# Last attention of a four-layer model: scores on 32-row tiles, value sums in nine rounds

## What is computed

```python
def _L3_attn_ref(x, W1, b1, W2, b2):
    y = jnp.einsum('bse,ef->bsf', x, W1) + b1
    y = y.reshape(B, S, H, -1).transpose(0, 2, 1, 3)
    q, k, v = jnp.split(y, 3, axis=-1)
    dk = jnp.asarray(v.shape[-1], x.dtype) ** 0.5
    w = jnp.einsum('bhqd,bhkd->bhqk', q, k) / dk
    mask = jnp.tril(jnp.ones((S, S), dtype=x.dtype))
    w = w * mask - NEG_BIG * (1.0 - mask)
    w = jax.nn.softmax(w, axis=-1)
    attn = jnp.einsum('bhqk,bhkd->bhqd', w, v)
    attn = attn.transpose(0, 2, 1, 3).reshape(B, S, E)
    return jnp.einsum('bse,ef->bsf', attn, W2) + b2
```

## Time and profile before

| | |
|---|---|
| runs | 1695.24, 1697.96, 1697.95 us |
| profiled execution | 1706.63 us, span 1704.9 |
| mean granted TensorE clock | 0.952 of 2.4 GHz |
| busy share of the span | PE 87%, DVE 74%, ACT 64%, POOL 50% |
| the stage that changes | from 1354 us to the end |

### The profile page before, as it was taken

How to read it: one execution, slowest core, us unless ns; L and a number is a source line. 1 busy time by engine, 2 the same in 40 slices (tenths; PEclk the granted TensorE clock), 3 DMA queues, 4 the chain that set the end, 5 groups by cost and what they waited for, 6 DMA issues and landing times. The chain is left out here.

```text
span 1704.9 us, 29946 instructions
## 1 busy us (share of the span) xinstructions
PE 1490.4 (87%) x11248; PEld 1197.3 (70%) x11248; DVE 1260.4 (74%) x2770; ACT 1089.9 (64%) x2122; POOL 857.1 (50%) x798
## 2 busy tenths in 40 slices
PE   6999999999999999899848888845999379998997
PEld 4788887888788887687737676834788256666675
DVE  6999999999999999435461677589433887777772
ACT  4888888888888888455445565632444456666665
POOL 4556576667666666720363744624666632233211
PEclk9999999999999999999779999957999699999999
DMA  3656666656666565300044000040465200000000
GB/s 94 124 103 115 106 120 100 120 108 114 115 108 103 99 105 106 87 1 1 18 137 129 26 2 2 2 133 1 112 148 109 64 1 1 2 2 2 2 2 26
DMA packets 334417, 117.09 MB, mean 69 GB/s; under 512 B 281008, under 2 KB 326096, under 8 KB 334144
## 3 DMA queue, kind: packets, MB, share of 16 engines
q1 hardware_dynamic: 323664, 101.54, 29.2%
q0 software_dynamic: 8496, 12.59, 3.4%
q10 hardware_dynamic: 2112, 1.05, 0.2%
HBM read 37.53 MB, written 10.49 MB: 28 GB/s over the span
## 5 line engine op out<-in xcount | busy, mean ns | idle before, releaser
L2135 ACT ACTIVATE ET_a<-PS 128x256 f32<-128x256 f32 (+2 forms) x512 | 220.5, 499 | 114.8 <-PE PS L2028 72.9
L771 POOL TENSOR_TENSOR dl<-XN,dh 128x1024 f16<-128x1024 f32 x86 | 184.9, 2150 | 155.2 <-DVE D L743 79.7
L205 PE MATMUL PS<-xh,yh 128*128 128x512 f32 x512 | 215.5, 421 | 6.6 <-ACT XNT L608 3.8
L206 PE MATMUL PS<-xl,yh 128*128 128x512 f32 x512 | 204.0, 398 | 0.0
L207 PE MATMUL PS<-xh,yl 128*128 128x512 f32 x512 | 202.8, 396 | 0.0
L608 ACT ACTIVATE G<-PS,nm 128x1024 f32<-128x1024 f32 x128 | 143.0, 1117 | 53.4 <-DVE nm L693 37.9
L608 ACT ACTIVATE XNT<-PS,nm 128x1024 f32<-128x1024 f32 x128 | 143.1, 1118 | 52.3 <-DVE nm L693 41.0
L687 DVE TENSOR_REDUCE nm<-PS 128x1 f32<-128x1024 f32 x128 | 156.6, 1223 | 15.7 <-PE PS L207 13.8
L689 DVE TENSOR_REDUCE nm<-PS 128x1 f32<-128x1024 f32 x128 | 156.0, 1219 | 4.7 <-PE PS L207 1.0
L205 PE MATMUL PS<-dth,xnh 128*128 128x256 f16 x512 | 141.0, 275 | 12.0 <-DVE zl L697 12.0
L2323 DVE CUSTOM_DVE_ANT_0 PS<-PS,mk 128x256 f32<-128x256 f32 (+3 forms) x256 | 128.2, 516 | 30.6 <-PE PS L2007 30.2
(11 more groups left out here) (461 smaller groups left out, 4091.1 us busy)
## 6 DMA issues: line engine op xcount, KB each, us to landing
e_wg<-in_WgT SPq DMA_DIRECT2D x16, 256.0 KB
e_wu<-in_WuT SPq DMA_DIRECT2D x16, 256.0 KB
e_wd<-in_WdT SPq DMA_DIRECT2D x16, 256.0 KB
dth<-dh SPq DMA_TRANSPOSE x128, 3.2
dtl<-dl SPq DMA_TRANSPOSE x128, 3.2
m_x_rows<-m_xs SPq DMA_DIRECT2D x1, 1472.0 KB, 4.9
m_xs<-m_x_rows SPq DMA_DIRECT2D x5, 256.0 KB, 4.8
m_y_rows<-m_xs SPq DMA_DIRECT2D x5, 256.0 KB, 2.3
```

What stands on the lines that cost most here:

```text
L205: e.matmul(o, l[0], r[0], start=start, stop=False)
L206: e.matmul(o, l[0], r[1], start=False, stop=False)
L771: e.tensor_tensor(self.dl[:, g % 4, :], self.D[g % 3], self.dh[:, g % 4, :], SUB).then_inc(*self.d_low.up(g))
L2135: e.activation(dst, src, ACT.Exp, scale=self.SC, bias=0.0).then_inc(*self.ex.up(it))
```

## The change

Keys are kept once, in `KA[:, n % 3, :]`, written by VectorE from the projection as the queries are. Row and column scores use partitions 32 hh to 32 hh + 31 alone, on the array tile at (32 hh, 0). The lag is 70 steps, so that the column scores in step x are those of head x - 5, at the same j. The value sums are nine rounds of four products, at j = 2, 3, 4, 5, 7, 8, 9, 10, 11; the first four wait only for the first diagonal mask. The row parts have a new order, and the second part of a long row takes the first part's result as the start of its minimum, so the merge goes. Side work is placed by a table of its own, ScalarE's take-out moves from j = 6 to 12, and the row score is issued ahead of the column score.

```diff
-        self.KH = [[sb(f"KH{n}_{i}", [128, 1024], F32R) for i in range(4)] for n in range(3)]
+        if kind == 3:
+            self.KA = sb("KA", [128, 3, 1024], F32R)
...
+            self.rparts += [firsts[0], firsts[1], seconds[0], firsts[2], seconds[1], firsts[3], seconds[2], seconds[3]]
...
-        self.AV_AT = (0, 4) if kind == 3 else (11, 12)
-        self.lag = 63 if kind == 3 else 70
-        self.av_parts = range(na // 2), range(na // 2, na)
+        self.AV_AT = (2, 3, 4, 5, 7, 8, 9, 10, 11) if kind == 3 else (11, 12)
+        self.lag = 70
+        self.av_parts = [range(n, n + 1) for n in range(na)] if kind == 3 else [range(na // 2), range(na // 2, na)]
...
-                m += [("max", n - 1, c) for c in range(2)]
-            if n + 1 < self.NQ and hh in (1, 2):
-                m += [("project", n + 1, w_, hh - 1) for w_ in (1, 0)]
+                m += [(1, ("max", n - 1, 0)), (5, ("max", n - 1, 1))]
+            if n + 1 < self.NQ:
+                m += {1: [(1, ("project", n + 1, 1, 0)), (8, ("project", n + 1, 0, 0))], 2: [(0, ("project", n + 1, 1, 1))],
+                      3: [(1, ("project", n + 1, 0, 1))]}.get(hh, [])
             if x - 7 >= 1 and (x - 7) % 2 and x - 7 < NH:
-                m += [("give", x - 7)]
+                m += [(8, ("give", x - 7))]
...
-            for ck in range(2):
-                self.spread_odd(e, q, ("project", 0, 1, ck))
...
-                t = e.matmul(o[:, 0:wd], qs[:, 128 * i:128 * i + 128], kh[:, c0:c0 + wd], start=True, stop=True)
+                r = slice(32 * hh, 32 * hh + 32)
+                t = e.matmul(o[:, 0:wd], qs[r, 128 * i:128 * i + 128], kh[r, c0:c0 + wd], start=True, stop=True, tile_position=(32 * hh, 0))
...
-                t = e.matmul(o[:, 0:wd], kh[:, 128 * jj:128 * jj + 128], qs[:, q1 - wd:q1], start=True, stop=True)
+                t = e.matmul(o[:, 0:wd], kh[r, 128 * jj:128 * jj + 128], qs[r, q1 - wd:q1], start=True, stop=True, tile_position=(32 * hh, 0))
...
+            q.wait_ge(self.cut, (x, int(part >= 4) if self.kind == 3 else 1))
             if part == 0:
-                q.wait_ge(self.cut, (x, 1))
...
-            if j == (6 if self.kind == 3 else 13) and 0 <= x - 6 < self.NH and x % 2:
+            if j == (12 if self.kind == 3 else 13) and 0 <= x - 6 < self.NH and x % 2:
...
+                to = self.KA[:, n % 3, cs] if w_ else self.QS[n % 3][:, cs]
+                e.scalar_tensor_tensor(out=to, in0=o, scalar=self.bq[:, w_, qd:qd + 1], in1=f(hn), op0=ADD,
                                        op1=SUB).then_inc(*self.mi.up(u))
...
+                    least = 3e38
+                    if c0:
+                        least = self.P2[:, n % 2, i - 4, hh:hh + 1]
+                        q.wait_ge(self.top, ("row", x, self.rparts.index((i, 0, c0, True))))
                     e.tensor_tensor_reduce(out=o[:, 0:c1 - c0], in0=o[:, 0:c1 - c0], in1=w.mk[:, 512 - (c1 - c0):512], scale=-1.0,
-                                           scalar=3e38, op0=ADD, op1=MIN, accum_out=dst).then_inc(*self.top.up(it))
-                if j == self.nr - 1:
-                    m4 = M[:, 4:8, col].rearrange("p i c -> p (i c)")
-                    q.wait_ge(self.top, it)
-                    e.tensor_tensor(m4, m4, self.P2[:, n % 2, :, hh], MIN).then_inc(*self.top.up(("both", x)))
+                                           scalar=least, op0=ADD, op1=MIN, accum_out=dst).then_inc(*self.top.up(it))
```

More of the change, by code:

```diff
@@ L1646, in __init__ @@
         self.scratch = None if kind == 3 else self.ET[1][:, :, :].rearrange("p j w -> p (j w)")[:, 0:1024]
-        self.KH = [[sb(f"KH{n}_{i}", [128, 1024], F32R) for i in range(4)] for n in range(3)]
+        if kind == 3:
+            self.KA = sb("KA", [128, 3, 1024], F32R)
+        else:
+            self.KH = [[sb(f"KH{n}_{i}", [128, 1024], F32R) for i in range(4)] for n in range(3)]
         edge = 64 if kind == 1 else 0
@@ L1663, in __init__ @@
             self.rparts, self.cparts = [], []
+            firsts, seconds = [], []
             for i in range(8):
@@ L1666, in __init__ @@
                 cut = 0 if w_ <= 512 else (384 if w_ == 640 else 512)
-                self.rparts += [(i, 0, cut, True)] * (cut > 0) + [(i, cut, w_, False)]
+                if cut == 0:
+                    self.rparts += [(i, 0, w_, False)]
+                else:
+                    firsts.append((i, 0, cut, True))
+                    seconds.append((i, cut, w_, False))
                 lo = 128 * i
@@ L1702, in __init__ @@
             if hh == 0 and 1 <= n <= self.NQ:
-                m += [("max", n - 1, c) for c in range(2)]
-            if n + 1 < self.NQ and hh in (1, 2):
-                m += [("project", n + 1, w_, hh - 1) for w_ in (1, 0)]
+                m += [(1, ("max", n - 1, 0)), (5, ("max", n - 1, 1))]
+            if n + 1 < self.NQ:
+                m += {1: [(1, ("project", n + 1, 1, 0)), (8, ("project", n + 1, 0, 0))], 2: [(0, ("project", n + 1, 1, 1))],
+                      3: [(1, ("project", n + 1, 0, 1))]}.get(hh, [])
             if x - 7 >= 1 and (x - 7) % 2 and x - 7 < NH:
-                m += [("give", x - 7)]
+                m += [(8, ("give", x - 7))]
             if x in (33, 35):
-                m += [("fin", (x - 33) // 2), ("finp", (x - 33) // 2)]
+                m += [(1, ("fin", (x - 33) // 2)), (4, ("finp", (x - 33) // 2))]
             elif x in (34, 36):
-                m += [("sum", (x - 34) // 2)]
-            for j, what in enumerate(m):
-                self.misc[x, 1 + 3 * j] = what
+                m += [(2, ("sum", (x - 34) // 2))]
+            for j, what in m:
+                self.misc[x, j] = what
         first = [("project", 0, w_, ck) for w_, ck in ((1, 0), (0, 0), (1, 1), (0, 1))]
@@ L1772, in __init__ @@
         self.row = k.sig("a_row", rows)
-        self.top = k.sig("a_row_max", [y for r in rows for y in ([r] + ([("both", r[1])] if kind == 3 and r[2] == self.nr - 1 else []))])
+        self.top = k.sig("a_row_max", rows)
         self.col = k.sig("a_col", cols)
@@ L1941, in maxima @@
             _, n, c = u
-            q.wait_ge(self.top, ("both", 4 * n + 3) if self.kind == 3 else ("row", 4 * n + 3, self.nr - 1))
+            q.wait_ge(self.top, ("row", 4 * n + 3, self.nr - 1))
             o = k.bank(self.side_of[u])
@@ L2054, in sums @@
                                      skip_group_check=True, tile_position=(0, 32 * g))
-            if part == 1:
+            if part == len(self.av_parts) - 1:
                 t.then_inc(*self.av.up(x))
@@ L2066, in pe @@
             y, m = divmod(14 * x + j - self.lag, 14)
+            if self.kind == 3 and j in self.at and x < self.NH:
+                row(x, self.at[j])
             if m in self.at and 0 <= y < self.NH:
                 col(y, self.at[m])
-            if j in self.at and x < self.NH:
+            if self.kind == 1 and j in self.at and x < self.NH:
                 row(x, self.at[j])
@@ L2091, in project @@
             high(u, o)
-            spread(u)
+            if self.kind == 1:
+                spread(u)
         def high(u, o):
@@ L2102, in high, with spread @@
             e.activation(hn, o, ACT.Identity, scale=m3[:, w_:w_ + 1], bias=self.bm[:, w_, qd:qd + 1]).then_inc(*self.mi_act.up(u))
-        def spread(u, heads=(0, 2)):
+        def spread(u):
             _, n, w_, ck = u
@@ L2108, in spread @@
                 q.wait_ge(self.mi, u)
-                for hh in heads:
+                for hh in (0, 2):
                     r = slice(32 * hh, 32 * hh + 32)
                     self.k_free(q, n, hh)
[L2112 to L2116, removed]
+                    to = self.KH[n % 3][hh][:, 512 * ck:512 * ck + 512]
+                    e.activation(to[r, :], f(hn[r, :]), ACT.Copy).then_inc(*self.k_act.up(("k", n, ck, hh)))
         def col(x, j):
@@ L2200, in hm_free @@
         _, n, w_, ck = u
-        if w_:
+        if w_ and self.kind == 1:
             q.wait_ge(self.k_act, ("k", n, ck, 2))
```

37 lines of the change are left out of this document (8 added, 29 removed).

## The result

The changed kernel takes 1885.47 us (median of 4 runs, 1881.26 to 1892.11) where the kernel before takes 1697.53 (4 runs, 1695.24 to 1697.96): ratio 1.1114, interval 1.1079 to 1.1149. It is 11% slower. The forecast was 1691, with a range up to 1726: it went the wrong way and far outside the range.

What follows compares the result with a forecast made beforehand. TensorE was taken as nearest to the bound. Stretches of -6, -3.3, -8.75, +0.6 and +10.2 made -7.2 us, from 1706.6 to 1699.4 profiled, hence a median of 1691; range 1664 to 1726.

Steps and rivals of the forecast that it cites:

- The clock: Rival for steady heads and tail: the granted clock falls to 0.89 throughout, 1727 us; chance 0.14.
- Pairs side by side: Slots of the last stage: row and column score run together, 2.64 us a head against 4.28, -1.64.
- Nine interruptions of 0.33: Value sums as nine rounds: each interruption costs TensorE 0.33 us, 2.97 a head against 0.66, +2.31.
- The rival in which they cost nothing: Value-sum rounds: interruptions cost next to nothing, VectorE bounds, -35 us, 1663 us; chance 0.14.
- Period of 37.4 at full clock: Four steady heads of the last stage take 37.4 us against 39.15, -1.75.
- Keys kept once: Heads 0 to 4: masked key copies and five merges go, -6 us (bounds 0 and -8).
- The rest of the sum: Last stage's other stretches: heads 5 to 7 -3.3 us, 8 to 27 -8.75, 28 to 31 +0.6, tail +10.2.

Runs made afterwards that it cites:

- the doubled kernel: The changed kernel with every value product issued twice and summed, against the kernel before: 1790.46 us (2 runs), ratio 1.0549.

## Why the prediction was wrong

**The step that failed** is the clock. The sum took the durations of the earlier trace rows, measured at a granted clock of 1.00, for the whole stage. The text had the rival ("The clock", chance 0.14), named the sign that would show it, and even the cause ("the new scores use a quarter of the rows"). But it priced it at 0.89, the mean of heads 0 to 4 in the earlier trace rows, and argued against it with "TensorE streams most of the time still". The runs refute just that argument. With 32-row scores the clock is low while TensorE is busy 39.92 of 40 us, and streaming twice as long left it there. What goes with the clock is how many of the array's rows the scores use, in every pair of runs above that differs in them: narrowed in the kernel before (1.00 to 0.59), widened again in the changed kernel (0.50 to 0.96), and 64 rows in between. And 0.89 was no floor: it was a mean over stretches at either level, and the new kernel never leaves the lower one between 1378 and 1868 us.

The Trainium skill ("TensorE: Matmul & The Clock Gate", section "What's actually happening") has the clock set by how busy TensorE has been. In the sense of busy time in the profile, this case doesn't agree: 488.23 of 490 us busy at 0.50.

**Pairs side by side: right.** Behind a round they start within 0.01, at the lower clock in the changed kernel and at the upper one with its value products doubled. The kernel before with 32-row scores shows the condition that the forecast gave, different quarters of the rows.

**Nine interruptions of 0.33: right** at full clock, by the head of 9.31 for 9.23 with whole-array scores and by 0.35 in the doubled kernel's slot with 32-row ones. The rival in which they cost nothing is refuted by both. The Trainium skill's rule that a change of tiling mode drains the engine ("TensorEngine Tiling (Array Packing)", "Key Properties") agrees with that head.

**Period of 37.4 at full clock: right** within 1%, by 37.7 worked out from the doubled kernel's 45.58. At half clock a period takes 62.56, which is 1.67 times the forecast and not 2: not everything in a slot goes with the array's clock (a slot is 0.80 at 1.00 and 1.31 at 0.50).

**Keys kept once: −4.0 for −6, near by luck.** Heads 0 to 4 gained 4.0 in spite of a clock of 0.76 for 0.89. The forecast gave the gain to the copies and the merge. But kernels that still make all four copies gain more. The stretch of heads 0 to 4 with the new order alone, with the new order, places, lag and row score first, and with the nine rounds as well:

```profile
1355.63:1400.97 45.34, 35.77 (x163) 26.70 (x162) 36.98 (x112) 26.14 (x48) 18.10 (x13) 0.85 0.00 1
```

```profile
1344.79:1382.37 37.58, 29.37 (x154) 22.37 (x154) 33.90 (x106) 23.33 (x41) 17.98 (x13) 0.91 0.00 1
```

```profile
1358.60:1396.28 37.68, 29.48 (x154) 22.41 (x154) 33.89 (x106) 23.31 (x41) 17.75 (x13) 0.91 0.00 1
```

That is +0.7, −7.1 and −7.0 against the 44.64 of the earlier trace rows, with the copies in place; leaving out the merge brings no gain by itself. Nor was the stretch before "row scores alone": its column scores begin at 1393.9 us, inside head 4, and with the lag of 70 they begin behind it. The gain goes with the side work's places (42.71 with them and the new order) and above all with the lag and the row score first. The changed kernel with two blocks, which makes no copies, has 37.82, so no run here shows a gain from the copies in these heads.

**The rest of the sum** went down with the clock: heads 5 to 7 +12.0 for −3.3, heads 8 to 27 +115.9 for −8.75, heads 28 to 31 and the tail +61.3 for +10.8. The sum of these misses, with 2.0 in heads 0 to 4 and 1.1 at the end, is 193.5 us: the measured +186.3 less the forecast's −7.2.

**How the loss divides.** Rows alone cost 7.6%, and the rounds alone 1.9%. Everything but the rows, with the key copies kept, costs 2.3% together. All together cost 11.1%, which is 1.2% more than 7.6% and 2.3%. That fits with rounds at half clock: two blocks for the nine rounds bring the changed kernel from 1.1114 to 1.0735, 3.8%, where nine rounds cost 1.9% at full clock in the old order and 1.0% in the new (1.0227 for 1.0131). Two things lie in that 3.8%, the interruptions that last longer and the short recoveries of the clock (0.60 for 0.50), and no run parts them.

**What stays open.** Why the doubled kernel stays at 0.50 until 1490 us and at about 1.00 from there on, with the same work per head. It rises right behind a doubled round and four transposes (1488.26 to 1490.34 us), which it had passed before at the lower level; so the rows in use don't settle the level by themselves. By what measure of rows and time the clock falls. Why the new order alone costs 0.4%, and lag with the row score first 0.8% more. What the 32-row form would do with its free rows filled by other useful work was not tried.

## What to carry to other kernels

A duration from a trace holds at the clock it was read at. Before work is moved to a part of the array's rows, price the forecast at both of TensorE's levels, and ask which whole-row work remains in the stage to hold the clock up. A low clock can stand beside a busy share of 100%, so "busy" is no argument that the clock will stay.

## What the runs showed of the hardware

- Granted clock by rows of the score, with only the scores changed: 0.59 with 32, 0.85 with 64, 1.00 with 128 (1500 to 1540 us), though the added rows multiply zeros.
- More work can take less time: value products doubled, 1790.46 us for 1885.47, because the clock rose from 0.50 to 0.99 behind 1490 us.
- Products in different quarters of the rows start 0.01 apart; in the same quarter 0.43, at the low clock and 512 columns.
- Nine changes in and out of the 32-column tiling in a head leave the clock at 1.00, with whole-array scores, and cost 0.33 us each.
